# Attention of a recurrent residual kernel: x's row chunks turned in units with four key blocks, the last sequence's own in its own last steps

## The reference

```
x = x + L0(x, cond)      # gated recurrence over 512 steps
x = x + L1(x, cond)      # tanh recurrence
x = x + L2(x, cond)      # tanh recurrence
qkv = x @ c_attn_w + c_attn_b                  # q, k, v; k and v get one image row in front
attn = softmax(mask(q k^T / sqrt(32)))         # key j is seen by row i if j <= i + 1
x = x + (attn @ v) @ c_proj_w + c_proj_b
```

## Time and profile before

| | us |
|---|---|
| median of 3 runs | 3827.79 (3826.57 to 3827.9) |
| the profiled execution's own time | 3826.17 |
| its span in the trace | 3824.5 |
| TensorE busy | 3746.8 (98%) |
| VectorE busy | 2358.2 (62%) |
| ScalarE busy | 1104.8 (29%) |

### The profile page before, as it was taken

How to read it: one execution, slowest core, us unless ns; L and a number is a source line. 1 busy time by engine, 2 the same in 40 slices (tenths; PEclk the granted TensorE clock), 3 DMA queues, 4 the chain that set the end, 5 groups by cost and what they waited for, 6 DMA issues and landing times. The chain is left out here.

```text
span 3824.5 us, 170528 instructions
## 1 busy us (share of the span) xinstructions
PE 3746.8 (98%) x77565; PEld 2492.1 (65%) x77565; DVE 2358.2 (62%) x8897; ACT 1104.8 (29%) x3969; POOL 39.6 (1%) x192
## 2 busy tenths in 40 slices
PE   7999999999999999999999999999998999999998
PEld 5777676766677767676667776767654555555555
DVE  3566666666666666666666666666645666666665
ACT  2211111111111111111111111111115665665565
POOL 0000000000000000000000000000000000000000
PEclk9999999999999999999999999999999999999999
DMA  4100000000000000000000000000010000000000
GB/s 172 36 4 4 3 4 3 4 3 3 4 3 4 3 4 3 3 4 3 4 3 3 3 4 4 3 4 3 36 38 4 12 10 12 15 13 15 12 7 20
DMA packets 34547, 47.18 MB, mean 12 GB/s; under 512 B 5856, under 2 KB 22288, under 8 KB 33824
## 3 DMA queue, kind: packets, MB, share of 16 engines
q1 hardware_dynamic: 31520, 29.96, 2.5%
q10 hardware_dynamic: 2304, 6.29, 0.4%
HBM read 27.86 MB, written 8.39 MB: 9 GB/s over the span
## 5 line engine op out<-in xcount | busy, mean ns | idle before, releaser
L253 PE MATMUL bank<-wh,h 128*16 128x256 f32 (+1 forms) x16960 | 982.6, 372 | 7.6 <-ACT h L352 6.9
L231 PE MATMUL bank<-wh,states 128*8 128x256 f32 x16352 | 976.1, 379 | 9.4 <-DVE states L481 9.4
L253 PEld LDWEIGHTS bank<-wh,h 128*16 128x16 f32 (+1 forms) x16960 | 487.0, 96 | 321.6 <-ACT h L352 25.1
L231 PEld LDWEIGHTS bank<-wh,states 128*8 128x8 f32 x16352 | 445.1, 90 | 346.1 <-DVE states L481 20.5
L453 DVE STREAM_TRANSPOSE tp<-bank 128x256 f32<-128x256 f32 x512 | 230.7, 451 | 605.2 <-PE bank L231 603.8
L237 PE MATMUL bank<-wh,states 128*8 128x128 f32 x16352 | 540.0, 273 | 0.0
L237 PEld LDWEIGHTS bank<-wh,states 128*8 128x8 f32 x16352 | 447.2, 90 | 108.1
L357 ACT ACTIVATE gates_sb<-pre_sb 128x32 f32<-128x32 f32 x512 | 117.5, 229 | 1207.9 <-DVE pre_sb L455 1207.9
L272 PE MATMUL bank<-probs_extra,w_qkv 128*32 128x128 f32 x11904 | 393.1, 273 | 0.0
L272 PEld LDWEIGHTS bank<-probs_extra,w_qkv 128*32 128x32 f32 x11904 | 339.9, 110 | 64.3
L352 ACT ACTIVATE h<-sum 128x64 f32<-128x64 f32 (+1 forms) x530 | 135.1, 255 | 775.0 <-DVE sum L405 775.0
(11 more groups left out here) (142 smaller groups left out, 3462.4 us busy)
## 6 DMA issues: line engine op xcount, KB each, us to landing
rows<-in_x_dram SPq DMA_DIRECT2D x32, 256.0 KB, 2.9
out_dram<-X SPq DMA_DIRECT2D x32, 256.0 KB, 2.6
w_qkv<-in_L_cond_c_attn_w_dram SPq DMA_DIRECT2D x1, 3072.0 KB, 11.4
w_qkv<-in_L_cond_w_W_dram ACTq DMA_DIRECT2D x4, 512.0 KB, 7.8
wh<-in_L_cond_w_W_dram ACTq DMA_DIRECT2D x4, 512.0 KB, 13.9
wx<-in_L_cond_Wx_dram SPq DMA_DIRECT2D x2, 1024.0 KB, 7.3
wh<-in_L_cond_Wh_dram SPq DMA_DIRECT2D x2, 1024.0 KB, 9.6
wx<-in_mask_Bx1x1xS_ff_dram SPq DMA_DIRECT2D x8, 256.0 KB, 3.2
```

The source lines that it names most:

```text
L231: mm = pe.matmul(mem.ps0[32 * j:32 * j + B, 0:2 * P], state[:, k, :], columns_of(mem.wh0[:, k, 0:3:2, :], j), start=(k == 0), stop=(k == K ...
L253: mm = pe.matmul(mem.ps12[32 * j:32 * j + B * len(ls), P * l0:P * l1], h12[:, k, (n - 1) % HR, l0:l1, :].rearrange("p l b -> p (l b)"), co ...
```

## The change

`rows` jobs move. Chunk 0 of a sequence is now turned in its own unit 13, chunks 1, 2 and 3 in units 1, 5 and 9 of the next sequence, all of them units whose turns have five rounds. There the `rows` job comes first: after two rounds of turns the `rows` job, then two more rounds, then the job that the step had (q in each case), then the last round. The last sequence now has `rows` jobs too: chunk 0 in unit 13, and 1, 2, 3 in units 11, 12 and 14. The identity matmuls of `project` are gone, and VectorE's last four additions add the projection to the rows in `mem.X`. VectorE keeps the `rows` chunk first, then q. `proj` jobs stand where they stood.

```diff
-ROWS_OF_LAST = {2: [("rows", 0)], 5: [("rows", 1)], 6: [("rows", 2)], 9: [("rows", 3)]}
+ROWS_OF_LAST = {1: [("rows", 1)], 5: [("rows", 2)], 9: [("rows", 3)]}
+ROWS_OF_OWN = {13: [("rows", 0)]}
+ROWS_AT_END = {11: [("rows", 1)], 12: [("rows", 2)], 14: [("rows", 3)]}
...
+def rows_of(i):
+
+    u, l = i // PER, i % PER
+    return [(u, *job) for job in ROWS_OF_OWN.get(l, [])] + [(u - 1, *job) for job in ROWS_OF_LAST.get(l, []) if u]
...
-    jobs = []
+    jobs = rows_of(i)
...
-    if u and l in ROWS_OF_LAST:
-        jobs += [(u - 1, *job) for job in ROWS_OF_LAST[l]]
+    if u == B - 1:
+        jobs += [(u, *job) for job in ROWS_AT_END.get(l, [])]
...
-                if residual:
-                    for k in range(KC):
-                        mm = pe.matmul(bank[:, k * P:(k + 1) * P], mem.X[:, k, u, tc * P:(tc + 1) * P],
-                                       mem.ident[:, :], start=False, stop=False, skip_group_check=True)
...
                 jobs = jobs_of(i) if i < UNITS else []
+                turned = 2
+                if jobs and rows_of(i):
+                    product(*jobs.pop(0))
+                    turn(i - 2, 2, 4)
+                    turned = 4
                 if jobs:
                     product(*jobs[0])
...
                 if 2 <= i < UNITS + 2:
-                    turn(i - 2, 2, None)
+                    turn(i - 2, turned, None)
...
                 elif kind == "rows":
-                    ins = keep_rows(u, c, bank)
+                    ins = nc.vector.tensor_tensor(rows_at(u, c), bank[:, :].rearrange("p (k c) -> p k c", k=KC),
+                                                  mem.bias_tiles[:, 1, :].rearrange("p (k c) -> p k c", k=KC), ALU.add)
...
-                keep_rows(B - 1, tc, mem.banks[tc]).then_inc(s.out_rows, 1)
+                add_rows(B - 1, tc, mem.banks[tc]).then_inc(s.out_rows, 1)
```

More of the change, by code:

```diff
@@ L832, in product @@
                     pe.wait_ge(s.weighed_kept, HG * (u + 1))
-                    mm = project(bank, u, c, range(HG), False)
+                    mm = project(bank, u, c, range(HG))
                 elif kind == "rows":
@@ L842, in product, with project @@
                 mm.then_inc(s.product_done, 1)
-            def project(bank, u, tc, groups, residual):
+            def project(bank, u, tc, groups):
                 for k in groups:
@@ L931, in _ @@
                     for tc in (0, 1) if i == UNITS else (2, 3):
-                        project(mem.banks[tc], B - 1, tc, range(HG - 1), True)
+                        project(mem.banks[tc], B - 1, tc, range(HG - 1))
                 if 2 <= i < UNITS + 2:
-                    turn(i - 2, 2, None)
+                    turn(i - 2, turned, None)
                 for job in jobs[1:]:
@@ L940, in _ @@
             for tc in range(QC):
-                project(mem.banks[tc], B - 1, tc, [HG - 1], False).then_inc(s.projected, 1)
+                project(mem.banks[tc], B - 1, tc, [HG - 1]).then_inc(s.projected, 1)
         @block.scalar
@@ L1026, in keep, with rows_at, add_rows @@
                 elif kind == "rows":
-                    ins = keep_rows(u, c, bank)
-                else:
-                    dve.wait_ge(s.product_kept, place[u, "rows", c] + 1)
-                    rows = mem.X[:, :, u, c * P:(c + 1) * P]
-                    ins = nc.vector.tensor_tensor(rows, bank[:, :].rearrange("p (k c) -> p k c", k=KC), rows, ALU.add)
+                    ins = nc.vector.tensor_tensor(rows_at(u, c), bank[:, :].rearrange("p (k c) -> p k c", k=KC),
+                                                  mem.bias_tiles[:, 1, :].rearrange("p (k c) -> p k c", k=KC), ALU.add)
+                else:
+                    ins = add_rows(u, c, bank)
                 ins.then_inc(s.product_kept, 1)
[L1034 to L1038, removed]
+            def rows_at(u, tc):
+                return mem.X[:, :, u, tc * P:(tc + 1) * P]
+            def add_rows(u, tc, bank):
+                dve.wait_ge(s.product_kept, place[u, "rows", tc] + 1)
+                return nc.vector.tensor_tensor(rows_at(u, tc), bank[:, :].rearrange("p (k c) -> p k c", k=KC),
+                                               rows_at(u, tc), ALU.add)
             def scores_of(i):
```

## The result

| | before | changed |
|---|---|---|
| median, us | 3827.89 (6 runs, 3826.57 to 3829.52) | 3845.12 (6 runs, 3837.26 to 3846.64) |
| profiled execution, its own time | 3826.17 | 3845.56 |
| its span | 3824.5 | 3843.7 |
| mean granted clock of its span | 0.998 | 0.995 |

The ratio is 1.0041 with a 95% interval from 1.0031 to 1.0051: slower, by more than the 0.2% that can be told from no change. The forecast was 3842 us, the range 3832 to 3851.

A forecast was written before the change was run, and what follows sets the result against it. TensorE, busy 98.01 of 100 us, was taken to bound the kernel. Terms of -20.7, +30.6, -3.6 and +8 (clock) gave +14.3 us: 3840.5 on the profiled execution, forecast 3842 us, range 3832 to 3851.

The forecast's parts named there:

- The stalls removed: Units 2 and 6: TensorE's stalls at the rows job go, 2.96 us per sequence, -20.7 us over 7 sequences.
- q waits for VectorE: Units 1, 5, 9, 13: q waits until VectorE, behind its scores block, has kept the rows; +30.6 us.
- The end: Last steps: four groups of identity matmuls leave TensorE's path, -3.56 us; the last sequence's new rows jobs cost 0.
- Sum without the clock: Whole kernel: -20.7 + 30.6 - 3.6 = +6.3 us.
- The clock: Unit 9: the clock falls behind five of six holes of 2.1 us, 1.6 us each, +8 us.
- The waits come, the clock stays: Rival: q's waits come but the clock does not fall at unit 9; +6.3, 3834 us, chance 0.2.
- The clock falls in all four kinds of unit: Rival: four in ten of the 21 places beside unit 9 also lose 1.7 us; +29, 3857 us, chance 0.1.
- Faster, because VectorE is not late: Rival: q does not wait in units 1, 5, 9, 13; -3.8 us per sequence, 3798 us, chance 0.07.
- turning point: Average wait of q below which the change turns from slower to faster: 1.05 us, against 1.3 expected.

The follow-up runs named there:

- mask work in unit 7: The changed kernel with VectorE's work on the next mask in unit 7 instead of unit 8; 3828.97 us, ratio 1.0004 to the kernel before.
- the move alone: The kernel before with rows jobs moved as in the change for sequences 0 to 6, identity matmuls kept at the end; 3841.64 us, ratio 1.0039.
- keeping early: The changed kernel with VectorE keeping the rows chunk ahead of the two operations that end its scores block; 3811.1 us, ratio 0.9955.
- Without the split: The changed kernel with q straight behind rows, ahead of the third and fourth round of turns; 3878.83 us, ratio 1.0132.

## Why the prediction was right

**The stalls removed.** Right: both waits of 5.5 us are gone.

**q waits for VectorE.** Right, and it is the cause of the loss in waits: shown three ways, by the wait itself, by q's start that does not move when two rounds are taken from before it (3.98 and 3.99 us), and by the wait that goes when VectorE keeps earlier. The terms, as distance from the unit's scores to q: forecast 3.97, 3.86, 5.16 and 3.86 us in units 1, 5, 9 and 13, measured 3130.26 - 3126.30 = 3.96, 3.98, 3187.84 - 3182.69 = 5.15 and 3217.47 - 3213.61 = 3.86. Unit 5 is off by 0.12 in this one, of sequence 2, since VectorE's second score read started that much later; in the six other sequences it is 3.85 or 3.86, as forecast. The difference per sequence is small and elsewhere. Each of the four units takes 0.03 to 0.05 us more than forecast (3.85 us from q to the weighing where I had 3.80), and each of the two removed stalls gives 1.44 for my 1.48. That makes +1.83 per sequence for my 1.59.

**The end.** Right: -3.4 us by itself, and -3.8 between two traces with the same number of low stretches. That the new jobs are covered by TensorE's waits follows from the same two numbers: without that cover it would be -1.8.

**Sum without the clock.** I had +6.3. The traces give 11.0 + 2.2 - 5.5 = +7.7. The two executions of the change at clock 0.998, the mean that the kernel before shows in half of its own, took 3837.3, or +9.4.

**The clock.** The mechanism was right, four falls at unit 9 for my five, 1.7 us each for 1.6, in both traces. It is shown by mask work in unit 7, in whose trace the long holes and all falls at unit 9 are gone. How many falls come was not forecast by anything but a guess, and the count differs by trace: four, four, and three in the move alone. What I did not foresee: the clock also fell between `hidden` 0 and `hidden` 1, 6.4 us in the first trace, and its low stretches in the last units were fewer by one or two.

**The number.** The trace's 19.2 us are 4.9 more than my 14.3: +1.4 in the sum without the clock, -1.1 at unit 9, +6.4 between `hidden` 0 and 1, +1.6 ahead of that, -3.4 in the last units. So the median came within 3 us partly by luck: 8 us that I had not foreseen were offset by 3.4 that I had not foreseen either, and both differ between executions. The q waits, the removed stalls, the end and the price of a fall are not luck; each was measured by itself.

**The rivals.** "The waits come, the clock stays" (3834 us) is what the fastest executions, at 3837 us, come near to; none of them has a trace. "The clock falls in all four kinds of unit" did not come: no fall at any hole of 0.7 to 0.8 us from sequence 1 on. That a page of the Trainium skill ("TensorE: Matmul & The Clock Gate", Part 4) does not count transposes as a busy TensorE in the way of other matmuls is not separated by these runs; in those units, four rounds of turns, the `rows` job and the hole did not lower the clock.

"Faster, because VectorE is not late" did not come, but its condition was the right one: with waits of 0.24 us on average (6.7 over 28) the same list on TensorE is 17 us faster than before. I had put its turning point at 1.05 us; with mask work in unit 7 the average is 0.7 by the profile, and the time is level with before, so it lies lower (my own terms average 1.2, and not the 1.3 that I wrote). Two reasons can be read off. The price was too high: where q does not wait, keeping early shows units 1, 5, 9 and 13 at +0.30, -0.24, -0.24 and +0.19 us against before (unit 9 of sequence 7), which with -2.88 for the two stalls is -2.9 per sequence for my -3.8, and by that sum the turning point is (7 x 2.9 + 3.5) / 28 = 0.85. And the profile counts a wait shorter than the starts do: between keeping late and early the start of q moves by 3.86 - 3.02 = 0.84 us in most units 5, where the hole is 0.68.

## What to carry to other kernels

Where jobs share one buffer, the job placed first must be one that the emptying engine can empty at once. Look at what that engine has queued before the emptying, in its own order, and not at its busy share: VectorE was idle a third of the time and still came 0.8 to 2.0 us late, because its scores block stood ahead. A short job whose emptying is late belongs behind a long one, whose own time covers VectorE's block. And a job's time does not include what the clock can add: behind a 2 us hole it fell in four of six cases, in two traces, at 1.7 us each.

## What was not expected of the hardware

Two things. First, a longer hole did not bring more falls. Without the split the hole in unit 9 is up to 3.0 us, and its trace has one fall in six such holes (at 3067 us), while the change, with 2.0 us, has four in both of its traces:

```profile
3064.00:3074.00 10.00, 7.03 (x26) 0.83 0.00 0
```

Other executions of that same kernel took 3883.45 and 3882.8 us at a mean clock of 0.994, against 3872.12 at 0.998. So whether a fall comes at a hole of 2 to 3 us differs by hole and by execution, and the number of falls at such holes can't be forecast from these runs. Times of such a kernel spread by 6 to 11 us, those of the kernel before by 3 to 6 on the same chips.

Second, the clock also fell with nothing but short holes before it. In sequence 0 the changed kernel lost the full clock three times, and once in the unit behind it, with no hole over 0.72 us just before, and the kernel before has the same hole in unit 4 at the full clock. Yet from sequence 1 on, 27 holes of 0.7 to 0.8 us in one trace brought no fall. What decides it was not tried.
